# One row buffer in place of two in a fused attention and expert block: the load of the rows, their statistics and four orders in the queues moved

## The chip, the cores and the metric

One core of one Trainium2 chip runs the whole program in one launch. The metric is the device time of an execution in microseconds (us), the median of the runs. The engines are TensorE (PE; PEld is its weight load), VectorE (DVE), ScalarE (ACT), GpSimd (POOL) and SyncE (SP), which here issues all transfers.

## The reference, cut to what matters

```python
x = x + tanh(g_xattn) * attention(layernorm(x), ctx)      # x: 16 batches of 256 rows, 512 wide; 16 heads of 32, causal
x = x + tanh(g_ffn) * experts(layernorm(x))               # softmax router, top 6 of 8 experts, plus a shared one
```

The kernel computes float32 products in three passes over high and low parts, so each operand that TensorE reads is written twice: a high part by ACT and the difference (the low part) by DVE or POOL.

## The kernel before, in words

The program has two halves. The attention half goes through the 16 batches in passes i = -1 to 16; the expert half follows from about 600 us on, and its first steps are woven into passes 14, 15 and 16. The change lies in the attention half.

**A pass.** Each pass has 16 slots s, one per head. Every engine runs the same double loop over passes and slots and does in each slot what its own list says; semaphores tie the engines together. Pass i computes the scores and the softmax of batch i (one head a slot), projects q, k and v for batch n = i + 1, finishes the output projection and the residual of batch o = i - 1, and loads and normalises the rows x of batch ln = i + 2. In order of the slots, as far as they matter here:

- SP: `turn` (L413) issues one transposing transfer of a head's probabilities a slot, two slots late. In slot 0 it stores the finished x1 of batch i - 2 (L424; in pass 16 this is in slot 2), in slot 1 it loads x of batch ln (L438, `X_LOAD`), in slot 2 x of batch o again as the residual (L433, `RES_LOAD`), in slot 9 the context (L445).
- PE: slots 0 and 2 transpose the normalised x of batch n (L780 from `x_in` or `x_odd`), slots 4 to 7 project q, 8 to 11 v, 12 to 15 the output (L790); every fourth slot has the scores of four heads (L896) and the values of four (L916 to L918).
- DVE: in slots 0, 4, 8 and 12 the maxima of four heads (L720), in slot 5 the statistics of x (L622 to L635: `bn_stats`, `bn_aggr` and four small instructions that end in a first guess of 1/std), in slot 6 a low part of q (L740) and the closing of four heads (L673, L674, L678), in slot 10 a rest of v (L728), another closing and the normalising of x (L642), in slot 11 the low part of the transposed values (L660), for which PE's output projection in slot 12 waits.
- ACT: a cast (L592) and two exponentials (L598) a head, and the high parts.
- POOL: a low part of the probabilities a head, one slot late (L488, "split" below), in slot 6 the residual plus bias (L504, two instructions), in slot 7 the eleven small steps that refine 1/std (L81, L83, "Newton steps" below, `NEWTON_SLOT`), in slots 11 and 13 a third part of v (L493).

**Two buffers.** x of even batches goes to `x_odd`, of odd ones to `x_in`. The load of batch ln therefore waits only for the transposes of batch i, which PE did in the pass before. `x_odd` lies in memory that later belongs to the experts; POOL (pass 15, slot 3) and ACT (pass 15, slot 1) wait for two semaphores before they write there for the experts: `scores_done` of batch 14 and `v3_made` of batch 15.

Pass -1 has its own list of slots (`First`): PE transposes batch 0 in slots 5 and 6, DVE has the statistics of batch 1 in slot 8.

Of the kernel before, what the change touches and what calls it, by code (L numbers as in the profile page):

```python
# [15 lines left out]
P = 128  # L16
# [84 lines left out]
class Attended(NamedTuple):  # L101
# [13 lines left out]
    pv_done: object  # L115
    v3_made: object

# [68 lines left out]
def attention(nc, ctx, memory, x, ctx_t, g_xattn, g_ffn, wq_t, wk_t, wv_t, wo_t, bo, x1, x1t, done, ident, gates, tanh_gates):  # L186
# [24 lines left out]
    even = heads_of(0)  # L211
    x_odd = sb("x_odd", [P, T, D])
    sb("experts_space", [P, 2 * JH * C * S - D - T * D])

    def x_of(n):
        return x_in if n.k % 2 else x_odd

    v_rest = [sb("v_rest0", [P, D])]
# [47 lines left out]
    x1_stored, x1t_stored, x1_made, x_hat_made, hat_t_made, scores_done, o_done, v_done = done[:8]  # L266
    q_done, xt_done, c_lo_made, max_made, pv_done, v3_made = done[8:]
    row_chain, guess2_made, pool_chain2 = sem("row_chain"), sem("guess2_made"), sem("pool_chain2")
# [3 lines left out]
    small_loaded = sem("small_loaded")  # L272
    x_loaded, c_loaded, res_loaded = [sem("even_x_loaded"), sem("odd_x_loaded")], sem("c_loaded"), sem("res_loaded")

    ident_made, mask_made, bias_made = sem("ident_made"), sem("mask_made"), sem("bias_made")
    pool_chain, rstd_made = sem("pool_chain"), sem("rstd_made")
    res_made = sem("res_made")
# [51 lines left out]
    X_T_LOADS = (1, 4, 6, 8)  # L329
    X_LOAD, RES_LOAD, C_LOAD, GATE_LOAD, ROWS_LOAD = 1, 2, 9, 12, 13  # L330
    LN_SLOT, NEWTON_SLOT, XN_SLOT = 5, 7, 10
    K_SLOTS, K_EVAC = (0, 1, 2, 3), (2, 4)
# [46 lines left out]
    def phase(i):  # L379

        return i.k - (B - 2)
# [3 lines left out]
    def build(start):  # L385
        def sync(sp):
            sp.dma_start(c_in[:], c_v[0]).then_inc(c_loaded, DMA)
            for n in range(N_RAW):
                src = w_v[RAW_ORDER[n // 2]][:, :, (n % 2) * HD:(n % 2 + 1) * HD]
                sp.dma_start(raw[n], src).then_inc(raw_loaded[n], DMA)  # L390
                if n == 1:
                    sp.dma_start(x_of(At(0, 2, 0))[:], x_v[0]).then_inc(x_loaded[0], DMA)
                    sp.dma_start(gates[:, 0:1], g_xattn.partition_broadcast(P)).then_inc(small_loaded, DMA)
                    sp.dma_start(gates[:, 1:2], g_ffn.partition_broadcast(P)).then_inc(small_loaded, DMA)
                    sp.dma_start(bias[:], bo.partition_broadcast(P)).then_inc(small_loaded, DMA)
# [20 lines left out]
            def run(i):  # L416
                n, o, ln = i + 1, i + -1, i + 2
                k = hat_tile(i + -1)
                for s in range(H):
                    if (bh := lagging(i, s, TURN_LAG)):  # L420
                        turn(head(*bh))
                    if s == (2 if is_end(i) else 0) and has(i, -2):
                        sp.wait_ge(x1_made, (i + -2).times(T, T))
                        sp.dma_start(row(x1_v, i + -2), x_res[:]).then_inc(x1_stored, DMA)  # L424
                    if s == 2 and k is not None and k % T == T - 1:
                        store_hat(k // T)
                    if s in X_T_LOADS and phase(i) == 0:
                        start.sync(sp, phase(i), X_T_LOADS.index(s))
# [7 lines left out]
                    if s == X_LOAD and has(i, 2):  # L436
                        wait(sp, xt_done, ln.times(T, -T))
                        sp.dma_start(x_of(ln)[:], row(x_v, ln)).then_inc(x_loaded[ln.k % 2], DMA)  # L438
                    if s == 3 and phase(i) == 2:
                        start.sync(sp, phase(i), 1)  # L440
# [10 lines left out]
        def gpsimd(pool):  # L451
# [30 lines left out]
            def run(i):  # L482
                n, o, ln = i + 1, i + -1, i + 2
                for s in range(H):
# [16 lines left out]
                    if s == RES_SLOT and has(i, -1):  # L501
                        pool.wait_ge(res_loaded, o.times(DMA, DMA))
                        for t in range(T):
                            pool.tensor_tensor(x_res[:, t, :], x_res[:, t, :], bias[:], ALU.add).then_inc(res_made, 1)  # L504
                    if s == (NEWTON_SLOT if i.k >= 0 else places(i).moments) and has(i, 2):
                        inverse_std(ln)
# [107 lines left out]
        def vector(dve):  # L614
# [3 lines left out]
            def statistics(ln):  # L618

                dve.wait_ge(x_loaded[ln.k % 2], DMA * (ln.k // 2 + 1))  # L620
                for t in range(T):
                    dve.bn_stats(stats[:, t, :], x_of(ln)[:, t, :]).then_inc(norm_chain, 1)  # L622
                dve.wait_ge(norm_chain, ln.times(NORM_STEPS, T))
# [14 lines left out]
            def normalise(ln):  # L638

                dve.wait_ge(rstd_made, ln.times(1, 1))  # L640
                for t in range(T):
                    dve.tensor_scalar(x_of(ln)[:, t, :], x_of(ln)[:, t, :], mv[:, t, 0:1], rstd[:, t:t + 1],  # L642
                                      ALU.subtract, ALU.mult).then_inc(xn_made, 1)
# [129 lines left out]
        def tensor(pe):  # L773
# [40 lines left out]
            def units(i, s):  # L814
                n, o = i + 1, i + -1
                first = isinstance(n.r, int) and n.k == 0
                if has(i, 1):
# [14 lines left out]
                    if s in places(i).x:  # L832
# [4 lines left out]
                        if t == 1:  # L837
                            pe.wait_ge(xt_lo_made, n.times(T, 1))
                        transpose_rows(lambda c: x_of(n)[:, t, c * P:(c + 1) * P], rows_ps).then_inc(xt_done, 1)
                    if s in places(i).q:  # L840
# [101 lines left out]
def experts(nc, ctx, x1, x1t, done, router, w_gate, w_up, w_down, out, ident, tanh_gates):  # L942
# [27 lines left out]
    x1_stored, x1t_stored, x1_made, x_hat_made, hat_t_made, scores_done, o_done, v_done = done[:8]  # L970
    q_done, xt_done, c_lo_made, max_made, pv_done, v3_made = done[8:]

# [398 lines left out]
    def start_gpsimd(pool, phase, s):  # L1371
# [4 lines left out]
        elif (phase, s) == (1, 3):  # L1376
            pool.wait_ge(scores_done, H * (B - 1))
            pool.wait_ge(v3_made, GROUPS * B)
            x_lo_by(pool, 0, B11)
# [18 lines left out]
    def start_scalar(act, phase, s):  # L1398
        if (phase, s) == (1, 1):
            act.wait_ge(scores_done, H * (B - 1))  # L1400
            act.wait_ge(v3_made, GROUPS * B)
            weights_hi(act, 0, (W_A,))
# [477 lines left out]
```

## Time and profile before

| what | value |
|---|---|
| median of 3 runs | 1864.12 us (1862.8 to 1864.49) |
| profiled execution, its own time | 1864.49 us |
| its span, first to last instruction | 1862.7 us |
| busy: PE, PEld, DVE, ACT, POOL | 96%, 80%, 76%, 52%, 50% of the span |
| mean granted TensorE clock | 0.986 of full |

The profile is of one execution. Its span is 1.8 us shorter than the time of the same execution. A busy share is a mean over two halves with different limits, so it is read by stretch.

### The profile page before, as it was taken

Reading aid. Unit: us, or ns where it says so; the run is one execution under the profiler, and the core shown is the slowest. Engines: PE = TensorE matmul, PEld = TensorE weight load, DVE = VectorE, ACT = ScalarE, POOL = GpSimd, SP = SyncE. Lnnn points to the kernel's source line nnn. Section 1 sums busy time; section 2 is a strip of 40 time slices with the busy share of each in tenths; the row PEclk is TensorE's granted clock in tenths of the full one; section 3 lists DMA queues with packets and bytes.
Section 4 is the critical chain, followed back from the end, with each engine's and each line's share of the span. In section 5 each row is a group of like instructions: output and inputs, shape, how many; then the busy total and the mean of one; then the engine's idle time right before and its main releaser. Section 6 shows DMA issues by size and latency. Waiting matters only on the chain.

```text
span 1862.7 us, 33757 instructions
## 1 busy us (share of the span) xinstructions
PE 1788.4 (96%) x11904; PEld 1494.0 (80%) x11904; DVE 1419.7 (76%) x3101; ACT 965.2 (52%) x2260; POOL 925.8 (50%) x1185
## 2 busy tenths in 40 slices
PE   6999999999997999999999999999999999999999
PEld 6878888878885778888778888878888887888887
DVE  5787777777779777777877777787777788777776
ACT  4888888888888433333534243343333444333431
POOL 4776777777678333443533334434343452333330
PEclk9999999999997999999999999999999999999999
DMA  5678887887887412121141221123212113211111
GB/s 157 129 151 166 151 169 160 167 156 144 182 170 145 146 57 80 46 80 46 46 147 46 80 71 54 52 73 113 80 46 80 45 57 106 87 46 57 46 46 46
DMA packets 301000, 182.84 MB, mean 98 GB/s; under 512 B 210080, under 2 KB 265376, under 8 KB 300832
## 3 DMA queue, kind: packets, MB, share of 16 engines
q1 hardware_dynamic: 300832, 180.69, 39.3%
q8 instruction: 95, 1.56, 0.3%
q14 instruction: 73, 0.60, 0.1%
HBM read 111.43 MB, written 18.87 MB: 70 GB/s over the span
## 4 chain that ended last, share of the span: by engine, by line
PE 70%; DVE 11%; POOL 9%; issue 6%; ACT 2%; DMA 1%; SPq 0%; DVEq 0%; POOLq 0%; ACTq 0%
PE gate_up L1293 31%; PE down L1810 18%; PE bank L790 14%; POOL halves L488 3%; DVE ops_lo L1150 2%; DVE acc L1661 2%; PE scores L896 2%; POOL hidden L1509 1%; PE y_values L918 1%; POOL x_res L504 1%; PE rows_t L780 1%; PE y_values L916 1%; DVE xo_lo L1095 1%; PE down L1774 1%; PE down L1789 1%
## 5 line engine op out<-in xcount | busy, mean ns | idle before, releaser
L1293 PE MATMUL gate_up<-xo_hi,ops_hi 128*128 128x512 f32 x1120 | 439.9, 393 | 13.0 <-DVE hidden L1269 4.4
L1293 PE MATMUL gate_up<-xo_lo,ops_hi 128*128 128x512 f32 x1120 | 436.1, 389 | 0.0
L1293 PE MATMUL gate_up<-xo_hi,ops_lo 128*128 128x512 f32 x1120 | 436.0, 389 | 0.0
L488 POOL TENSOR_TENSOR halves<-probs,halves 128x384 f16<-128x384 f32 x244 | 228.8, 952 | 88.9 <-ACT halves L592 88.7
L1661 DVE SCALAR_TENSOR_TENSOR acc<-down,scale,acc 128x512 f32<-128x512 f32 x320 | 238.2, 745 | 34.8 <-PE down L1810 34.3
L1293 PEld LDWEIGHTS gate_up<-xo_hi,ops_hi 128*128 128x128 f32 x1120 | 210.2, 188 | 66.6 <-DVE gated L1269 9.5
L598 ACT ACTIVATE probs<-probs,neg_max 128x128 f32<-128x128 f32 (+1 forms) x512 | 228.9, 449 | 44.4 <-DVE neg_max L720 44.3
L1509 POOL TENSOR_TENSOR hidden<-hidden,gated 128x512 f32<-128x512 f32 x120 | 157.2, 1318 | 190.0 <-DVE hidden L1274 170.5
L1810 PE MATMUL down<-d_hi,h_hi 128*128 128x512 f32 x640 | 249.1, 389 | 0.0
L1810 PE MATMUL down<-d_lo,h_hi 128*128 128x512 f32 x640 | 249.1, 389 | 0.0
L1810 PE MATMUL down<-d_hi,h_lo 128*128 128x512 f32 x640 | 249.0, 389 | 0.0
L1293 PEld LDWEIGHTS gate_up<-xo_lo,ops_hi 128*128 128x128 f32 x1120 | 210.2, 188 | 44.1
L1293 PEld LDWEIGHTS gate_up<-xo_hi,ops_lo 128*128 128x128 f32 x1120 | 210.3, 188 | 42.4
L1544 ACT CAST h_hi<-hidden 128x512 fp32r<-128x512 f32 x160 | 95.3, 621 | 199.1 <-DVE hidden L1646 118.6
L1159 POOL TENSOR_TENSOR w_sums<-u_raw 128x256 f32<-128x256 f32 x40 | 29.5, 737 | 320.1 <-DVE ops_lo L1150 314.0
L1252 ACT COPY first<-gate_up 128x512 f32<-128x512 f32 x80 | 47.0, 587 | 260.9 <-PE gate_up L1293 260.9
L720 DVE CUSTOM_DVE_ANT_0 probs<-scores,mask 128x128 f32<-128x128 f32 (+1 forms) x512 | 147.3, 351 | 29.4 <-PE scores L896 26.1
L1533 ACT ACTIVATE gated<-gated 128x512 f32<-128x512 f32 x120 | 75.8, 632 | 147.9 <-DVE gated L1274 116.2
L1159 POOL TENSOR_TENSOR w_sums<-g_raw 128x256 f32<-128x256 f32 x40 | 36.6, 916 | 224.0 <-DVE ops_lo L1150 223.8
L1650 DVE TENSOR_TENSOR h_lo<-hidden,h_hi 128x512 fp32r<-128x512 f32 x160 | 117.3, 750 | 33.0 <-ACT h_hi L1544 32.8
L1810 PEld LDWEIGHTS down<-d_hi,h_hi 128*128 128x128 f32 x640 | 120.1, 188 | 25.3
L1810 PEld LDWEIGHTS down<-d_hi,h_lo 128*128 128x128 f32 x640 | 120.1, 188 | 25.0
(186 smaller groups left out, 4262.8 us busy)
## 6 DMA issues: line engine op xcount, KB each, us to landing
g_raw<-in_w_gate SPq DMA_DIRECT2D x40, 512.0 KB, 3.5
u_raw<-in_w_up SPq DMA_DIRECT2D x40, 512.0 KB, 3.5
d_raw<-in_w_down SPq DMA_DIRECT2D x40, 512.0 KB, 3.5
c_in<-in_ctx_t SPq DMA_DIRECT2D x16, 512.0 KB, 4.5
x_res<-in_x SPq DMA_DIRECT2D x16, 512.0 KB, 5.6
x_between<-x_res SPq DMA_DIRECT2D x16, 512.0 KB, 3.4
acc<-x_between SPq DMA_DIRECT2D x32, 256.0 KB, 4.4
out<-acc SPq DMA_DIRECT2D x32, 256.0 KB, 3.3
```

The lines of the kernel that those rows point to most:

```text
L488: pool.tensor_tensor(halves[k % HALVES][:, 1, :], probs[k % RING][:], halves[k % HALVES][:, 0, :], ALU.subtract).then_inc(p_lo_made, 1)
L598: ins = act.activation(p, p, ACT.Exp, bias=neg_max[:, s, t:t + 1], scale=-1.0, accum_out=row_sum[:, s, t:t + 1])
L720: ins = dve.tensor_tensor_reduce(probs_of(k, t), scores_of(k, t), mask[:, P * (1 - t):], -SCALE, -NEG, ALU.add, ALU.min, neg_max[:, h, t:t ...
L790: ins = pe.matmul(dst, stationary[a](c), moving[b](c), start=(c == 0 and k == 0), stop=(c == C - 1 and k == len(PASSES) - 1))
L1159: pool.tensor_tensor(w_sums[:, 0], a21, a22, ALU.add).then_inc(w_sum_made, 1)
L1293: ins = pe.matmul(gu_ps[bank][:], ops[x][:, which, a, c, :], xo[y][:, b, c, :], start=(begins and c == 0 and i == 0), stop=(c == CH - 1 an ...
L1509: pool.tensor_tensor(hidden[:, blk, :], hidden[:, blk, :], gated[:, blk, :], ALU.mult).then_inc(gated_made, 1)
L1533: act.activation(gated[:, blk, :], gated[:, blk, :], ACT.Silu).then_inc(silu_made, 1)
L1544: act.copy(h_hi[:, blk, :], hidden[:, blk, :]).then_inc(h_hi_made, 1)
L1650: dve.tensor_tensor(h_lo[:, blk, :], hidden[:, blk, :], h_hi[:, blk, :].bitcast(F32), ALU.subtract).then_inc(h_lo_made, 1)
L1661: dve.scalar_tensor_tensor(out=part, in0=ring("down", m, t)[:], scalar=scale[:, q, t, e:e + 1], in1=part, op0=ALU.mult, op1=ALU.add).then_ ...
L1810: ins = pe.matmul(ring(*use)[:], h[x][:, FC * g + f, t * P:(t + 1) * P], (d_hi, d_lo)[y][m % 2][:, f, :], start=(f == 0 and i == 0), stop= ...
```

## The change

- `x_odd` and its semaphore go; all batches use `x_in`. The memory around it stays where it was.
- SP issues the load of x of batch i + 2 in slot 3 behind the residual's load, where it was in slot 1 ahead of it, and waits before it for the transposes of batch i + 1, PE's slot 2 of the same pass.
- The statistics of x move from slot 5 to slot 7 of DVE. POOL's Newton steps stay in slot 7 (in pass -1 both stay in slot 8).
- In pass 16 the store of x1 of batch 14 moves from slot 2 to slot 0 of SP, that is, between the last two `turn`s.
- ACT and POOL no longer wait themselves for `v3_made` and `scores_done` in pass 15. SP does, in slot 1 after its `turn`, and then raises `early_free`, for which they wait.

```diff
-    x_odd = sb("x_odd", [P, T, D])
-    sb("experts_space", [P, 2 * JH * C * S - D - T * D])
-    def x_of(n):
-        return x_in if n.k % 2 else x_odd
+    sb("experts_space", [P, 2 * JH * C * S - D])
...
-    X_LOAD, RES_LOAD, C_LOAD, GATE_LOAD, ROWS_LOAD = 1, 2, 9, 12, 13
-    LN_SLOT, NEWTON_SLOT, XN_SLOT = 5, 7, 10
+    RES_LOAD, X_LOAD, C_LOAD, GATE_LOAD, ROWS_LOAD = 2, 3, 9, 12, 13
+    LN_SLOT, XN_SLOT = 7, 10
...
-                    if s == (2 if is_end(i) else 0) and has(i, -2):
+                    if s == 0 and has(i, -2):
                         sp.wait_ge(x1_made, (i + -2).times(T, T))
                         sp.dma_start(row(x1_v, i + -2), x_res[:]).then_inc(x1_stored, DMA)
...
+                    if s == 1 and is_last(i):
+                        sp.wait_ge(v3_made, T * B)
+                        sp.wait_ge(scores_done, H * (B - 1))
+                        sp.sem_inc(early_free, 1)
...
                     if s == X_LOAD and has(i, 2):
-                        wait(sp, xt_done, ln.times(T, -T))
-                        sp.dma_start(x_of(ln)[:], row(x_v, ln)).then_inc(x_loaded[ln.k % 2], DMA)
-                    if s == 3 and phase(i) == 2:
+                        sp.wait_ge(xt_done, ln.times(T))
+                        sp.dma_start(x_in[:], row(x_v, ln)).then_inc(x_loaded, DMA)
+                    if s == X_LOAD and phase(i) == 2:
...
-                    if s == (NEWTON_SLOT if i.k >= 0 else places(i).moments) and has(i, 2):
+                    if s == places(i).moments and has(i, 2):
                         inverse_std(ln)
...
-            pool.wait_ge(scores_done, H * (B - 1))
-            pool.wait_ge(v3_made, GROUPS * B)
+            pool.wait_ge(early_free, 1)
             x_lo_by(pool, 0, B11)
...
-            act.wait_ge(scores_done, H * (B - 1))
-            act.wait_ge(v3_made, GROUPS * B)
+            act.wait_ge(early_free, 1)
             weights_hi(act, 0, (W_A,))
```

## Rows read from the trace of the kernel before

**Rows 1.** The page: the chain that ended last, by engine.

```profile
PE 70%; DVE 11%; POOL 9%; issue 6%; ACT 2%; DMA 1%; SPq 0%; DVEq 0%; POOLq 0%; ACTq 0%
```

**Rows 2.** Windows: length, busy PE, PEld, DVE, ACT, POOL, clock, DMA share, GB/s.

```profile
182.97:219.58 36.61, 34.91 (x406) 30.71 (x406) 28.15 (x105) 30.04 (x96) 27.43 (x48) 0.95 0.92 157
219.58:254.73 35.15, 33.47 (x406) 29.66 (x406) 28.19 (x105) 29.96 (x96) 27.43 (x48) 1.00 0.79 148
```

**Rows 3.** Waits in 0 to 640 us: total, times, longest.

```profile
PE bank L790 <- DVE t_lo L660: 21.8, 15, 1.7
...
POOL x_res L504 <- DMA x_res<-in_x: 4.5, 2, 4.0
```

**Rows 4.** Timeline of pass 3, DVE: start, duration, what, [idle before <- releaser].

```profile
152.87 0.17 DVE L629 TENSOR_SCALAR var_eps<-mv 128x2 f32<-128x2 f32 x1
...
153.35 0.68 DVE L740 TENSOR_TENSOR q_lo<-bank,q_hi 128x512 fp32r<-128x512 f32 x1
...
154.74 1.06 DVE L678 TENSOR_TENSOR y<-y_sum,row_inv 128x256 f32<-128x256 f32 x1
156.21 0.29 DVE L720 CUSTOM_DVE_ANT_0 probs<-scores,mask 128x128 f32<-128x128 f32 x1 [0.41 <-PE scores L896]
...
162.54 0.91 DVE L678 TENSOR_TENSOR y<-y_sum,row_inv 128x256 f32<-128x256 f32 x1
163.38 2.19 DVE L642 TENSOR_SCALAR x_in<-x_in,mv,rstd 128x512 f32<-128x512 f32 x2
165.49 0.68 DVE L660 TENSOR_TENSOR t_lo<-rows_t,t_hi 128x512 fp32r<-128x512 f32 x1
```

**Rows 5.** The same pass on ACT.

```profile
156.89 0.41 ACT L598 ACTIVATE probs<-probs,neg_max 128x128 f32<-128x128 f32 x1 [0.36 <-DVE neg_max L720]
...
160.53 0.58 ACT L556 CAST v_parts<-bank 128x512 bf16<-128x512 f32 x1 [0.59 <-PE bank L790]
```

**Rows 6.** The same pass on POOL.

```profile
156.91 0.92 POOL L488 TENSOR_TENSOR halves<-probs,halves 128x384 f16<-128x384 f32 x1
157.79 0.20 POOL L83 TENSOR_TENSOR newton<-rstd 128x2 f32<-128x2 f32 x1
...
161.37 3.92 POOL L488 TENSOR_TENSOR halves<-probs,halves 128x384 f16<-128x384 f32 x4
```

**Rows 7.** PE's output projection in pass 3.

```profile
166.22 0.50 PE L790 MATMUL bank<-w_hi,t_hi 128*128 128x512 f32 x1 [1.66 <-DVE t_lo L660]
```

**Rows 8.** Pass 14, which has no statistics, on DVE.

```profile
547.48 1.52 DVE L678 TENSOR_TENSOR y<-y_sum,row_inv 128x256 f32<-128x256 f32 x1
```

**Rows 9.** Pass 2, whose slot 8 is late, on ACT and DVE.

```profile
123.56 0.40 ACT L598 ACTIVATE probs<-probs,neg_max 128x128 f32<-128x128 f32 x1 [1.96 <-DVE neg_max L720]
...
126.22 0.57 ACT L556 CAST v_parts<-bank 128x512 bf16<-128x512 f32 x1
...
129.31 1.59 DVE L642 TENSOR_SCALAR x_odd<-x_odd,mv,rstd 128x512 f32<-128x512 f32 x2
```

**Rows 10.** The tile `x_in`: durations in ns, min/median/max, first and last start.

```profile
L642 DVE TENSOR_SCALAR x_in<-x_in,mv,rstd x16: 535/1132/1352, 37.2 to 523.0; 128x512 f32<-128x512 f32 x16
...
DMA to landing us min/median/max: 4.3/5.0/8.7
```

**Rows 11.** SP's `turn` in slot 3 of pass 3.

```profile
147.28 1.21 SPq L413 DMA_TRANSPOSE turned<-halves  x1
```

**Rows 12.** Pass 15 on ACT, SP and PE.

```profile
570.65 0.60 ACT L1140 CAST ops_hi<-g_raw 128x512 fp32r<-128x512 f32 x1
...
573.96 1.56 SPq L413 DMA_TRANSPOSE turned<-halves  x1
...
582.27 1.12 PE L780 MATMUL rows_t<-ident,y 128*128 128x128 f32 x4 [2.46 <-DVE y L678]
...
589.43 0.80 PE L790 MATMUL bank<-w_hi,t_hi 128*128 128x512 f32 x1 [1.06 <-DVE t_lo L660]
```

**Rows 13.** PE's wait for the last transposed head, in pass 16.

```profile
606.50 0.20 PE L916 MATMUL y_values<-v_parts,turned 128*128 128x64 bf16 x1 [2.43 <-DMA turned<-halves]
```

More of the change, by code:

```diff
@@ L115 @@
     pv_done: object
-    v3_made: object
+    early_free: object
 class Slots(NamedTuple):
@@ L266, in attention @@
     x1_stored, x1t_stored, x1_made, x_hat_made, hat_t_made, scores_done, o_done, v_done = done[:8]
-    q_done, xt_done, c_lo_made, max_made, pv_done, v3_made = done[8:]
+    q_done, xt_done, c_lo_made, max_made, pv_done, early_free = done[8:]
     row_chain, guess2_made, pool_chain2 = sem("row_chain"), sem("guess2_made"), sem("pool_chain2")
@@ L272, in attention @@
     small_loaded = sem("small_loaded")
-    x_loaded, c_loaded, res_loaded = [sem("even_x_loaded"), sem("odd_x_loaded")], sem("c_loaded"), sem("res_loaded")
+    x_loaded, c_loaded, res_loaded = sem("x_loaded"), sem("c_loaded"), sem("res_loaded")
     ident_made, mask_made, bias_made = sem("ident_made"), sem("mask_made"), sem("bias_made")
-    pool_chain, rstd_made = sem("pool_chain"), sem("rstd_made")
+    pool_chain, rstd_made, v3_made = sem("pool_chain"), sem("rstd_made"), sem("v3_made")
     res_made = sem("res_made")
@@ L391, in sync @@
                 if n == 1:
-                    sp.dma_start(x_of(At(0, 2, 0))[:], x_v[0]).then_inc(x_loaded[0], DMA)
+                    sp.dma_start(x_in[:], x_v[0]).then_inc(x_loaded, DMA)
                     sp.dma_start(gates[:, 0:1], g_xattn.partition_broadcast(P)).then_inc(small_loaded, DMA)
@@ L618, in statistics @@
             def statistics(ln):
-                dve.wait_ge(x_loaded[ln.k % 2], DMA * (ln.k // 2 + 1))
+                dve.wait_ge(x_loaded, ln.times(DMA, DMA))
                 for t in range(T):
-                    dve.bn_stats(stats[:, t, :], x_of(ln)[:, t, :]).then_inc(norm_chain, 1)
+                    dve.bn_stats(stats[:, t, :], x_in[:, t, :]).then_inc(norm_chain, 1)
                 dve.wait_ge(norm_chain, ln.times(NORM_STEPS, T))
@@ L641, in normalise @@
                 for t in range(T):
-                    dve.tensor_scalar(x_of(ln)[:, t, :], x_of(ln)[:, t, :], mv[:, t, 0:1], rstd[:, t:t + 1],
+                    dve.tensor_scalar(x_in[:, t, :], x_in[:, t, :], mv[:, t, 0:1], rstd[:, t:t + 1],
                                       ALU.subtract, ALU.mult).then_inc(xn_made, 1)
@@ L838, in units @@
                             pe.wait_ge(xt_lo_made, n.times(T, 1))
-                        transpose_rows(lambda c: x_of(n)[:, t, c * P:(c + 1) * P], rows_ps).then_inc(xt_done, 1)
+                        transpose_rows(lambda c: x_in[:, t, c * P:(c + 1) * P], rows_ps).then_inc(xt_done, 1)
                     if s in places(i).q:
@@ L970, in experts @@
     x1_stored, x1t_stored, x1_made, x_hat_made, hat_t_made, scores_done, o_done, v_done = done[:8]
-    q_done, xt_done, c_lo_made, max_made, pv_done, v3_made = done[8:]
+    q_done, xt_done, c_lo_made, max_made, pv_done, early_free = done[8:]
     x_t = sb("x_t", [P, GROUPS, C, BLK])
```

## The prediction

> **What bounds the kernel now.** I read the page first: PE is busy 96% of the span, and most of the chain that ended last is PE's work, with DVE and POOL behind it [rows 1]. Such a chain says that PE is the bound with short waits in between, so the waits come next: in the attention half PE's one wait that comes back pass after pass is that of the output projection for the low part of the transposed values, 15 times up to 1.7 us [rows 3, 7]. The windows say what the rest of a pass is: about 35 us long and PE busy nearly throughout; in 5 of the 12 passes 2 to 13 the clock is 0.95 and the pass 1.5 us longer [rows 2]. In those five the clock falls to 1.2 GHz right behind that wait and comes back. So this change is priced by one question: when does DVE write that low part (L660), measured against PE?
>
> I then follow pass 3 back from it. L660 stands behind the normalising, 163.38 to 165.57; that behind a closing at 162.54; that behind ACT's high part of v at 160.53, for which ACT waited 0.59 us for PE [rows 4, 5]. ACT's exponential of slot 8 at 156.89 waited for DVE's maxima, which began at 156.21, 0.68 earlier, and these waited 0.41 for PE's scores [rows 4, 5]. Between slots 7 and 8 DVE thus has 0.41 us of air, and ACT 0.59 us behind it. In slot 5, where the statistics stand now, DVE's next work is a low part whose source ACT had finished 0.5 us before it began: air for a quarter of the 2.2 us.
>
> **The steady passes, step by step.** The statistics leave slot 5 and the low part of q begins 0.5 us earlier. That brings nothing, because the closing behind it ends in the multiplication L678, which is held by POOL's residual additions: in pass 14, with no statistics at all, it begins 0.46 us earlier in its pass and takes 1.52 us where pass 3 has 1.06 [rows 4, 8]: the end is the same. So in pass 3 it still ends at 155.80, and the statistics follow from 155.72 (neighbours overlap by 0.08).
>
> Their small instruction L629 comes 1.73 us after the start of the statistics, at 157.45. POOL is then in a split, 156.91 to 157.83 [rows 6]. DVE instructions of this kind are held until POOL's ends, as the second of pass 3's normalisings shows: 2.19 us for two that take 0.535 each at best [rows 4, 10]. So L629 ends at about 157.85, and the maxima begin 0.31 later as now from its end (153.04) to the next work (153.35) [rows 4]: 158.16 for 156.21, 1.95 us late. If POOL did not hold it, 1.7.
>
> ACT's exponential begins at 158.84. From there to the high part of v ACT needs 2.66 us if it waits for nothing, which pass 2 shows, where slot 8 was late already (123.56 to 126.22) [rows 9]. That gives 161.50 for 160.53: 0.97 late, the air taken off. The closing's multiplication, 2.01 behind it, is ready at 163.50 for 162.54. POOL's Newton steps begin when the guess is there, 158.35 for 157.79, and their four splits begin 3.58 later, at 161.93 for 161.37 [rows 6]. Splits and DVE's instructions now take turns: the multiplication gets in when the second split ends (163.73) and ends at 164.0; the third split ends at 164.8; the first normalising ends at 165.07; the fourth split, ready at 164.86, goes next and ends at 165.85; the second normalising ends at 166.13. L660 follows, and PE begins at 166.79 for 166.22: 0.57 us a pass. Only part of the 0.97 comes through, since DVE loses less to POOL than now. The bounds: 0.97 if it loses as much; and if the second normalising gets in ahead of the fourth split, as in pass 2 (1.59 us for both) [rows 9], L660 is at 165.4 and the pass gains 0.1. I take 0.57, as the fourth split is ready 0.2 us before the first normalising ends.
>
> The Trainium skill (SBUF — State Buffer, Who interferes with whom) has the rule behind this: VectorE and GpSimd share a port pair that is held for a whole instruction, and whichever issues first gets it. By it the fourth split goes first here too, but two instructions of VectorE back to back could keep the pair, and the sum would then lose its 6.3 us below.
>
> Passes with this shape are 1, 3 to 9 and 11 to 13: 11 x 0.57 = 6.3 us. Pass 2 is partly there already: 0.3. Pass 10 is late now from a wait of POOL for the residual's load, which the new order issues earlier [rows 3]; I count it as no change. Pass 0 has no output projection: 0.3, between 0 and 0.57. In pass -1 SP's new wait ends with PE's slot 6, ahead of DVE's slot 8; nothing. Sum 6.9; bounds -1.3 and 12.
>
> **The load.** It is issued behind SP's `turn` of slot 3, which ends at 148.5 in pass 3 [rows 11]; the transposes it waits for are over by then in every pass from 0 on (PE's slot 2). With 5.0 us to landing, at most 8.7 [rows 10], it is there at 153.5, and the statistics want it at 155.72: hidden under 2.2 us. The queue behind it, `turn`s of slots 4 and later, gains 0.7 us in slots 2 and 3 and loses it after; heads 0 to 3 are wanted in slot 9.
>
> **Pass 15.** ACT casts its first expert weights at 570.65. `early_free` comes after SP's `turn` in slot 1, issued from 573.96 to 575.52 [rows 12], because that `turn` waits for POOL's and DVE's splits and stands behind the store of x1. ACT stands still for 4.9 us. Behind it are its casts and exponentials of all later slots, and for them DVE's splits, SP's `turn`s and PE's transposes wait. ACT had hardly any air up to slot 11: PE's output projection at 589.43 waited for L660 and thus for ACT. I take 4.3 us; the bounds are 2.6, what I get by way of DVE's split of slot 6 to PE's transposes at 582.27, which waited for DVE already [rows 12], and 4.9. POOL's slot 3 is later than 575.5 and waits for nothing.
>
> **Pass 16.** The store of x1 now stands between the last two `turn`s: 0.6 us of issue and 512 KB ahead of the last head's transfer, for which PE already waits 2.43 us [rows 13]. All of it shows: 1.0 us, between 0.6 and 2.
>
> **The clock.** PE's wait grows from 1.7 to 2.3 us, and in pass 15 there is more idle time; I expect one more fall, 1.5 us, between none and eight (12 us, every pass).
>
> Sum: 6.9 + 4.3 + 1.0 + 1.5 = 13.7. Against the profiled execution's own 1864.49 (0.4 above the median, which I leave in) that is 1878.
>
> **Rivals.**
> - *Both costs as above*: 1878, with its own range 1873 to 1884. Chance 0.60.
> - *The full 0.97 comes through and the clock falls in half of the other passes or more*: 11 x 0.97 = 10.7 + 0.6 + 5.3, and 4 to 8 falls: 1887 to 1893. For it: the wait comes near what pass 15 has, where the clock is low; against: passes with 1.7 us escape 7 times of 12. 0.12.
> - *The load lands late* in the eight passes where DMA is busiest (share 0.92 at most) [rows 2]: a us each, 1886. The Trainium skill (DMA: Bandwidth & Descriptors, Rules for kernel authors) says to issue early and wait late, which the change does the other way; the rows above leave it 2.2 us of cover. 0.05.
> - *Only the end costs*: the second normalising slips in ahead of the fourth split, each pass gains 0.1: 1864.5 - 1.1 + 5.3 = 1869. 0.10.
> - *Nothing shows*: that, and ACT's stall is caught up before 589: 1864.5 - 1.1 + 1.0, 1864. 0.06.
> - *Faster*: both normalisings find POOL waiting for ACT's casts. Decided by whether the third split ends before the first normalising is ready (163.9; I have 164.8). They would take 1.1 instead of 2.19 us: 12 x 1.1 = 13.2 gained, 5.3 lost: 1857. 0.07.
>
> **How the numbers follow.** No change can be told from one below 0.2% (3.7 us). Slower: 0.60 + 0.12 + 0.05 + 0.10 = 0.87; same 0.06; faster 0.07. The range from 1867 to 1889 leaves out the last two cases and the upper half of the second.
>
> **What would show it.** In pass 3's counterpart: DVE's maxima of slot 8 follow the statistics with no wait, 1.9 us later in the pass; ACT waits some 2 us before the exponential of slot 8; PE's wait for L660 is 2.2 to 2.3 us; passes 35.2 us long, or 36.7 with a fall. In pass 15 ACT's first expert cast has 4.9 us of idle time before it. In pass 16 PE's wait for the last head is 3 us or more. I am wrong if PE's wait stays 1.7 us, or if the time lies in the first passes or in the expert half.

## The result and the profile after

| kernel | median | runs | ratio to before, 95% interval |
|---|---|---|---|
| before | 1862.8 us | 1858.96 to 1864.49, 5 runs | |
| after | 1873.6 us | 1871.63 to 1873.64, 5 runs | 1.0056 [1.0042, 1.0072] |

The change makes the kernel slower by 0.56%, 10.4 us by the ratio (the two medians are 10.8 apart). The prediction had 1878 in a range from 1867 to 1889. The profiled execution of after has a span of 1869.7 us, that of before 1862.7. These two are only 7.0 us apart: the profiled execution of after took 1871.45 us, less than any of its five in the table, that of before 1864.49, the most of its five, so what is read from the two traces adds up to less than the medians.

The page of after, the chain that ended last, by engine, as in [rows 1]:

```profile
PE 69%; DVE 15%; issue 6%; ACT 4%; POOL 3%; DMA 2%; SPq 1%; DVEq 0%; POOLq 0%; ACTq 0%
```

Windows of passes 4 and 5 of after, columns as in [rows 2]:

```profile
182.93:218.65 35.72, 33.71 (x406) 29.52 (x405) 28.09 (x105) 29.89 (x96) 27.48 (x47) 1.00 0.85 158
218.65:254.40 35.75, 33.78 (x406) 29.57 (x405) 28.68 (x105) 29.74 (x96) 27.41 (x48) 1.00 0.82 155
```

Waits of after from 0 to 640 us, as in [rows 3]:

```profile
PE bank L789 <- DVE t_lo L659: 16.7, 15, 1.3
...
PE bank L789 <- DVE q_lo L739: 10.9, 13, 1.6
```

Two things are to be seen. Each pass is 0.6 us longer than its counterpart (35.75 for 35.15), yet pass 4 is 0.9 us shorter than before, since its clock doesn't fall; none of the passes 1 to 13 has a fall now, and five had one before. And the wait for the low part of the transposed values has shrunk to 1.2 us, while a new one has come, for the low part of q. The waits together grew by 0.3 us a pass; the other 0.3 shows as busy time of PE (33.78 for 33.47 us, the same 406 products), and no run says why.

Pass 3 of after, timeline of DVE, the counterpart of [rows 4]:

```profile
153.57 1.51 DVE L677 TENSOR_TENSOR y<-y_sum,row_inv 128x256 f32<-128x256 f32 x1
155.00 1.27 DVE L621 BATCH_NORM_STATS2 stats<-x_in 128x6 f32<-128x512 f32 x2
...
156.73 0.41 DVE L628 TENSOR_SCALAR var_eps<-mv 128x2 f32<-128x2 f32 x1
...
157.57 0.29 DVE L719 CUSTOM_DVE_ANT_0 probs<-scores,mask 128x128 f32<-128x128 f32 x1
...
159.80 0.69 DVE L739 TENSOR_TENSOR q_lo<-bank,q_hi 128x512 fp32r<-128x512 f32 x1
...
162.90 0.43 DVE L677 TENSOR_TENSOR y<-y_sum,row_inv 128x256 f32<-128x256 f32 x1
163.24 2.22 DVE L641 TENSOR_SCALAR x_in<-x_in,mv,rstd 128x512 f32<-128x512 f32 x2
165.38 0.68 DVE L659 TENSOR_TENSOR t_lo<-rows_t,t_hi 128x512 fp32r<-128x512 f32 x1
```

The same pass on ACT, POOL and PE, as in [rows 5 to 7]:

```profile
158.25 0.40 ACT L597 ACTIVATE probs<-probs,neg_max 128x128 f32<-128x128 f32 x1 [2.43 <-DVE neg_max L719]
...
160.91 0.56 ACT L555 CAST v_parts<-bank 128x512 bf16<-128x512 f32 x1
...
157.62 0.20 POOL L83 TENSOR_TENSOR newton<-rstd 128x2 f32<-128x2 f32 x1 [0.51 <-DVE rstd L634]
...
161.22 2.88 POOL L487 TENSOR_TENSOR halves<-probs,halves 128x384 f16<-128x384 f32 x3
164.26 0.92 POOL L487 TENSOR_TENSOR halves<-probs,halves 128x384 f16<-128x384 f32 x1 [0.16 <-ACT halves L591]
...
160.54 0.50 PE L789 MATMUL bank<-w_hi,c_hi 128*128 128x512 f32 x1 [0.75 <-DVE q_lo L739]
...
166.12 0.50 PE L789 MATMUL bank<-w_hi,t_hi 128*128 128x512 f32 x1 [1.23 <-DVE t_lo L659]
```

Pass 3 of after began 0.72 us earlier (maxima of slot 4 at 147.59 for 148.31), so 0.72 is added to compare. The maxima of slot 8 are then 2.08 us late, the exponential 2.08, the high part of v 1.10, PE's output projection 0.62.

The end of the attention half, passes 15 and 16 of after, on ACT, SP and PE, as in [rows 12, 13]:

```profile
574.26 0.62 ACT L1139 CAST ops_hi<-g_raw 128x512 fp32r<-128x512 f32 x1 [4.88 <-SPq L425]
...
571.92 0.57 SPq L419 DMA_DIRECT2D x_between<-x_res  x1
572.60 3.00 SPq L408 DMA_TRANSPOSE turned<-halves  x2
...
605.69 0.57 SPq L419 DMA_DIRECT2D x_between<-x_res  x1
606.37 1.56 SPq L408 DMA_TRANSPOSE turned<-halves  x1
...
583.33 0.47 PE L779 MATMUL rows_t<-ident,y 128*128 128x128 f32 x1 [4.43 <-DVE y L677]
...
592.91 0.79 PE L789 MATMUL bank<-w_hi,t_hi 128*128 128x512 f32 x1 [1.31 <-DVE t_lo L659]
...
612.05 0.20 PE L915 MATMUL y_values<-v_parts,turned 128*128 128x64 bf16 x1 [4.38 <-DMA turned<-halves]
...
621.93 0.47 PE L1292 MATMUL gate_up<-xo_hi,ops_hi 128*128 128x512 f32 x1 [1.16 <-DVE xo_lo L1094]
```

To read the end apart from the passes, both kernels are measured from the same instruction, the first maxima of slot 4 of pass 14. In after:

```profile
540.31 0.29 DVE L719 CUSTOM_DVE_ANT_0 probs<-scores,mask 128x128 f32<-128x128 f32 x1 [1.18 <-PE scores L895]
```

In before, with the first product of the expert half on PE:

```profile
541.51 0.29 DVE L720 CUSTOM_DVE_ANT_0 probs<-scores,mask 128x128 f32<-128x128 f32 x1 [1.18 <-PE scores L896]
...
615.03 0.47 PE L1293 MATMUL gate_up<-xo_hi,ops_hi 128*128 128x512 f32 x1 [1.42 <-DVE xo_lo L1095]
```

After reaches pass 14 sooner than before, by 1.2 us. From there the output projection of pass 15 comes 52.6 us on for 47.9, the first product of the experts 81.6 for 73.5, the end of the span 1329.4 for 1321.2. So in this pair of traces all of the loss lies from pass 14 on: 8.2 us, of which the earlier start of pass 14 gives 1.2 back. The experiments show how much of that is the change, and why the longer passes don't show.

### The profile page after: what moved, and what is told of

Its sections match the earlier page's. It is cut to its first block, busy times and chain, and to the rows that moved or that the text cites. A ratio compares the mean times of both kernels' runs of the same rounds, so it can differ in the third digit from the quotient of the medians.

```text
span 1869.7 us, 33758 instructions
## 1 busy us (share of the span) xinstructions
PE 1785.5 (95%) x11904; PEld 1488.6 (80%) x11904; DVE 1420.5 (76%) x3101; ACT 963.3 (52%) x2260; POOL 926.1 (50%) x1185
## 4 chain that ended last, share of the span: by engine, by line
PE 69%; DVE 15%; issue 6%; ACT 4%; POOL 3%; DMA 2%; SPq 1%; DVEq 0%; POOLq 0%; ACTq 0%
PE gate_up L1292 32%; PE down L1807 19%; PE bank L789 13%; DVE ops_lo L1149 2%; DVE acc L1658 2%; ACT probs L597 2%; POOL hidden L1506 1%; PE scores L895 1%; DVE y L677 1%; DVE x_in L641 1%; PE y_values L917 1%; DVE stats L621 1%; PE rows_t L779 1%; PE y_values L915 1%; DVE y_sum L673 1%
## 5 line engine op out<-in xcount | busy, mean ns | idle before, releaser
L1807 PEld LDWEIGHTS down<-d_lo,h_hi 128*128 128x128 f32 x640 | 120.1, 188 | 25.1
```

The lines of the kernel that those rows point to most:

```text
L1807: ins = pe.matmul(ring(*use)[:], h[x][:, FC * g + f, t * P:(t + 1) * P], (d_hi, d_lo)[y][m % 2][:, f, :], start=(f == 0 and i == 0), stop= ...
```

## The experiments

All times are medians, each kernel run beside the kernel before on the same chip. "To the end" is the stretch of the profiled execution from the maxima of slot 4 of pass 14 to the end of the span.

| run | what it is | ratio, 95% interval | to the end |
|---|---|---|---|
| e1_end_only | before, both end edits | 1.0040 [1.0027, 1.0053] | 1330.2 |
| e2_stats_only | before, statistics in slot 7 | 1.0005 [0.9997, 1.0014] | 1322.7 |
| e3_after_direct_wait | after without `early_free` | 1.0023 [1.0014, 1.0032] | 1324.1 |
| e4_before_normalise_11 | before, normalising in slot 11 | 0.9915 [0.9901, 0.9928] | 1323.6 |
| e5_after_store_late | after, store of x1 in slot 2 | 1.0041 [1.0029, 1.0053] | 1328.5 |
| e6_load_order | before, load of x moved alone | 1.0123 [1.0108, 1.0137] | 1322.5 |
| e7_single_wait_longer | before, more DVE work in slot 10 | 1.0014 [1.0002, 1.0026] | 1321.9 |
| e8_after_no_end_normalise_11 | after, no end edits, normalising in 11 | 0.9978 [0.9970, 0.9987] | 1323.5 |
| e9_after_no_end | after, no end edits | 1.0019 [1.0010, 1.0028] | 1322.6 |
| e10_split_wait | before, more DVE work in slot 8 | 0.9997 [0.9988, 1.0006] | 1323.1 |
| e11_before_normalise_12 | before, normalising in slot 12 | 0.9917 [0.9904, 0.9931] | 1323.1 |
| e12_one_buffer_8_12 | one buffer, slots 8 and 12 | 0.9940 [0.9928, 0.9952] | 1326.8 |

### The end against the passes

`e1_end_only` and `e2_stats_only` put one part each into the kernel before. First e1, whose two edits are shown one below the other (ACT and POOL wait for `early_free`, as in after), then e2:

```diff
+                    if s == 1 and is_last(i):
+                        sp.wait_ge(v3_made, T * B)
+                        sp.wait_ge(scores_done, H * (B - 1))
+                        sp.sem_inc(early_free, 1)
...
-                    if s == (2 if is_end(i) else 0) and has(i, -2):
+                    if s == 0 and has(i, -2):
```
```diff
-    LN_SLOT, NEWTON_SLOT, XN_SLOT = 5, 7, 10
+    LN_SLOT, NEWTON_SLOT, XN_SLOT = 7, 7, 10
```

> The kernel before (two buffers, load and statistics where they were) with the two edits at the end of the attention half alone: SP raises early_free in slot 1 of pass 15, and the store of x1 in pass 16 stands between the last two turns. My theory now, from the profile after: these two carry all of the loss, because ACT stands still for 4.9 us before its first expert cast and PE waits 2 us longer for the last head. It expects 7 to 8.5 us over before, the first maxima of pass 14 where they are in the kernel before. Rival A, that the steady passes carry it (my forecast put 6.9 us there), expects 4 to 5.5 us over before. Rival B, that the end only costs in company of the later passes, expects under 2.

> The kernel before with one number changed: the statistics of x in slot 7 of DVE in place of slot 5; two buffers and the early load stay. Theory: this alone makes the steady pass of the kernel after, 35.2 us without and 35.8 us with the second layernorm's work (34.7 and 35.2 before), since L660 is 0.6 us later; PE's one wait of 1.7 us becomes two, 0.75 and 1.2 us, and the clock stops falling, which gives 5 x 1.5 us back. So the time is within 2 us of before, and the first maxima of pass 14 come at 540 to 542 us. Rival A, the clock falls are chance and come back: 6 to 8 us over before. Rival B, the later load and not the statistics makes the pass longer: pass length as before, 34.7 us, and the time within 1 us.

Measured: 1871.69 and 1864.76 us. The end edits alone are 7.5 us, with the same stall of ACT (4.87 us for 4.88) and the same wait of PE for the last head (4.30 for 4.38) as in after. The statistics alone are within 0.2% of before. But their passes show the price in full, 35.25 and 35.72 us, and PE's two waits:

```profile
PE bank L790 <- DVE t_lo L660: 16.3, 15, 1.2
...
PE bank L790 <- DVE q_lo L740: 9.8, 13, 0.9
```

Thirteen passes at 0.6 are paid back by the clock, which falls in none of the passes 1 to 13. This is not the luck of one trace: over all runs the mean granted clock is 0.991 in the 11 of e2 and 0.986 in the 21 of before beside it. The difference is 0.0046 of the span, 8.6 us of full clock, and five falls of 3.4 us at half speed are 8.5.

### Which end edit

`e3_after_direct_wait` takes `early_free` out of after (the edit of ACT is shown, POOL has the same), `e5_after_store_late` puts the store back:

```diff
-            act.wait_ge(early_free, 1)
+            act.wait_ge(scores_done, H * (B - 1))
+            act.wait_ge(v3_made, GROUPS * B)
```
```diff
-                    if s == 0 and has(i, -2):
+                    if s == (2 if is_end(i) else 0) and has(i, -2):
```

> The kernel after, with ACT and POOL waiting themselves for scores_done and v3_made in pass 15, and no early_free. Theory: ACT's 4.9 us of standing still go, PE's output projection of pass 15 comes 4.7 us earlier against pass 14, and the kernel gains 4.5 to 5.5 us on after. Rival A, PE's low clock in pass 15 and DVE's backlog make that up: a gain of 1 to 3 us. Rival B, the stall was on no path: no gain.

> The kernel after, with the store of x1 in pass 16 back in slot 2, behind the last head's transfer; early_free stays. Theory: the store's issue and bytes ahead of the last transfer cost what PE's wait for the last head grew by, 4.38 for 2.43 us in the kernel after (the first run of the end edits alone had 4.30). So that wait goes back to 2.4 to 2.8, and the time falls by 2 us against the kernel after, to about 1.0045 of before; the stall of 4.9 us before ACT's first expert cast stays. Rival: the wait for the last head grew because the whole chain of pass 15 to 16 is late and the transfers collide with others: then it stays above 4 us and the time stays at 1.0056 of before, within 0.1%.

Measured: 1868.19 and 1872.24 us. Without `early_free` ACT goes straight on (no idle time stands in its row) and the wait for the last head stays; with the late store it is the other way round. ACT and PE of `e3_after_direct_wait`:

```profile
571.73 0.60 ACT L1136 CAST ops_hi<-g_raw 128x512 fp32r<-128x512 f32 x1
...
609.41 0.24 PE L912 MATMUL y_values<-v_parts,turned 128*128 128x64 bf16 x1 [4.27 <-DMA turned<-halves]
```

The same of `e5_after_store_late`:

```profile
576.88 0.62 ACT L1139 CAST ops_hi<-g_raw 128x512 fp32r<-128x512 f32 x1 [4.88 <-SPq L425]
...
612.96 0.20 PE L915 MATMUL y_values<-v_parts,turned 128*128 128x64 bf16 x1 [2.67 <-DMA turned<-halves]
```

The two costs are apart: the early store makes the last wait (4.3 to 4.4 us with it in e1, e3 and after, 2.4 to 2.7 without it in before, e5 and e9), whatever came before it. With `e9_after_no_end`, where both are undone, four corners are measured:

> The kernel after with both edits at the end undone: ACT and POOL wait themselves for what early_free stood for, and in pass 16 the store of x1 is in slot 2. What is left is the steady part: one buffer, the load in slot 3 behind the transposes, the statistics in slot 7. Theory: the end edits alone gave 1.0040 and the statistics in slot 7 alone 1.0005, the kernel after 1.0056; what remains for the load in slot 3 is 0.0011, 2 us, which is pass 6, where x lands late. So 1865 to 1867, ratio 1.0005 to 1.0015, passes of 35.25 and 35.75 us and no or one fall of the clock in passes 1 to 14. Rival: the steady part costs what the prediction had, 8 us with the clock: 1872.

It came out at 1866.24 us, within the theory's times, its ratio just above them. To the end it is 1322.6 with neither, 1324.1 with the early store, 1328.5 with `early_free`, 1329.4 with both: about 1.2 us for the store and 5.6 for `early_free`. By the ratios the store is 0.7 to 2.8 us and `early_free` 4.1 to 6.1, and the steady part of the change, which alone is left here, costs 3.5 us (1.9 to 5.2).

### The load alone

```diff
-    X_LOAD, RES_LOAD, C_LOAD, GATE_LOAD, ROWS_LOAD = 1, 2, 9, 12, 13
+    X_LOAD, RES_LOAD, C_LOAD, GATE_LOAD, ROWS_LOAD = 3, 2, 9, 12, 13
...
-                        wait(sp, xt_done, ln.times(T, -T))
+                        wait(sp, xt_done, ln.times(T))
```

> The kernel before with two buffers, statistics in slot 5; only the load of x moves, to slot 3 behind the residual's load and behind the transposes of slot 2. Theory: the residual's load gains what x's load loses, the statistics in slot 5 begin 4 us after the load's issue and would now wait for it: landing 5 to 6 us after 148.5 in pass 3 is 153.5 to 154.5, while the statistics begin at about 151. So here the order alone does cost: DVE waits 2 to 3 us in slot 5 in every pass, of which PE has 0 to 2 us, 1865 to 1885. That gives the price of a load that lands late, which in the kernel after the statistics in slot 7 avoid in all passes but 6. Rival: DVE has air in slots 5 and 6 and the time stays within 0.1% of before.

Measured: 1887.58 us, just above the theory's bound. Pass 3 on SP, DVE and PE:

```profile
152.15 0.57 SPq L438 DMA_DIRECT2D x_in<-in_x  x1
...
157.09 1.29 DVE L622 BATCH_NORM_STATS2 stats<-x_in 128x6 f32<-128x512 f32 x2 [2.66 <-DMA x_in<-in_x]
...
158.83 1.15 DVE L629 TENSOR_SCALAR var_eps<-mv 128x2 f32<-128x2 f32 x1
...
161.70 0.50 PE L790 MATMUL bank<-w_hi,c_hi 128*128 128x512 f32 x1 [2.49 <-DVE q_lo L740]
```

DVE waits 2.66 us for x, a small instruction behind it takes 1.15 for 0.17 us, and PE waits 2.49 us for the low part of q. Passes 3 to 13 are 37.0 to 38.1 us, and the clock falls in 12 of the passes 1 to 13. The statistics in slot 7 are thus no extra cost but what makes the late load bearable: without them the steady part of the change would cost 23 us.

### Is the clock set by the length of the wait?

Two kernels give DVE more work in the kernel before, e7 ahead of the normalising, e10 behind the maxima of slot 8:

```diff
+                    if s == places(i).normal and has(i, 0) and has(i, 2):
+                        dve.bn_stats(unused[:], x_of(ln)[:, 0, :])
```
```diff
+                    if s == 8 and has(i, 0) and has(i, 2):
+                        for t in range(T):
+                            dve.bn_stats(unused[:, t, :], x_of(ln)[:, t, :])
```

> The kernel before with one more bn_stats of half of x, into a tile that nothing reads, ahead of the normalising in slot 10 (passes 0 to 14 that normalise). The output stays the reference's. PE's wait for the low part of the transposed values grows by 0.7 us, from 1.7 to 2.3 or 2.4, as one wait. In the kernel after the idle time is the same in sum but lies in two waits of 0.75 and 1.2 us, and the clock falls in none of passes 1 to 14. Theory: the single wait is what lets the clock fall in 5 passes of before; a longer single wait then falls in as many passes or more (5 to 12), and the time is 14 x 0.65 = 9 us plus 0 to 10 us: 1873 to 1883. Rival: whether the clock falls does not hang on the length of this wait: no more than 5 falls, and 1868 to 1873.

> The kernel before with more work and nothing else: two bn_stats of x into a tile that nothing reads, 1.2 us of DVE ahead of the low part of q in slot 8, in passes 0 to 13. The output stays the reference's. DVE has 1.43 us of idle time behind that low part and the next one, before the rest of v. Theory: PE must wait 0.5 to 0.7 us for the bank of v's second half, what comes behind it on DVE is where it was, and PE's later wait for the low part of the transposed values shrinks by the same: two waits of 0.6 and 1.1 us in place of one of 1.66, passes as long as before (34.65 and 35.15), and the clock then falls in none or one of passes 1 to 14, where before has 4 to 6 falls of 1.5 us: 1856 to 1859, faster for more work. Rival: the clock does not hang on how the waits are cut, and falls 4 to 6 times as before: 1862 to 1866. Second rival: the idle time is not there, and each pass grows by 0.3 or more: 1868 or more.

Measured: 1866.58 and 1862.43 us. Both theories missed (1873 to 1883 and 1856 to 1859), because neither kernel did to PE's wait what it was made for, so neither settles the question by itself. In e7 the extra instruction was nearly free. DVE in its pass 3:

```profile
161.61 0.93 DVE L679 TENSOR_TENSOR y<-y_sum,row_inv 128x256 f32<-128x256 f32 x1
162.46 0.68 DVE L768 BATCH_NORM_STATS2 unused<-x_in 128x6 f32<-128x512 f32 x1
163.06 1.59 DVE L643 TENSOR_SCALAR x_in<-x_in,mv,rstd 128x512 f32<-128x512 f32 x2
164.58 0.68 DVE L661 TENSOR_TENSOR t_lo<-rows_t,t_hi 128x512 fp32r<-128x512 f32 x1
```

The two normalisings take 1.59 for 2.19 us [rows 4]: what DVE had lost to POOL's splits was filled with work, and the low part comes as early as before. PE's wait stays 1.68 in pass 3 and about 1.7 in most others; only in passes 8 and 9 was it longer, 2.48 in both, and the clock fell in the second alone. That is good evidence for the step of the prediction by which lateness ahead of the normalising is partly swallowed, since the splits set its end. In e10 the wait was cut in passes 3 (0.61 and 0.74 us) and 4 (0.20 and 0.88), with no fall there; in the eleven others one wait of about 1.5 us stayed, and the clock fell in four of them. The second rival of e10, that there is no idle time to use, is out: 1.2 us more of work a pass cost nothing.

What bears on it most is all traces together. For passes 1 to 13 of the 14 kernels, the longest wait of PE in the pass, and whether the clock falls in it:

| longest wait of PE in the pass | passes | with a fall |
|---|---|---|
| up to 1.3 us | 114 | 0 |
| 1.3 to 2.0 us | 51 | 17 |
| over 2.0 us | 17 | 15 |

So up to 1.3 us the clock never fell here, and above 2.0 nearly always. Between them the length doesn't decide: in before, the five passes with a fall had waits of 1.63 to 1.71 us, seven without one 1.65 to 1.70. What decides among those is open.

### A better place for the normalising

The first edit is of the kernel before (e4; in e11 the last number is 12), the second of after with both end edits undone (e8; in e12 the numbers are 8 and 12):

```diff
-    LN_SLOT, NEWTON_SLOT, XN_SLOT = 5, 7, 10
+    LN_SLOT, NEWTON_SLOT, XN_SLOT = 5, 7, 11
```
```diff
-    LN_SLOT, XN_SLOT = 7, 10
+    LN_SLOT, XN_SLOT = 7, 11
```

> The kernel before with the normalising of x in slot 11 of DVE, behind the low part L660, in place of slot 10, ahead of it. A measure of what PE's steady wait for L660 is worth. Theory: L660 begins 2.1 us earlier, PE's wait of 1.7 us falls below 0.3 us in passes 1 to 13 and with it the five falls of the clock: 13 x 1.5 + 5 x 1.5, 22 to 28 us under before. Rival A, the maxima of slot 12 are then late and PE waits for ACT elsewhere: 5 to 12 us under before. Rival B, the clock falls stay although the wait is gone: 17 to 20 us.

> One buffer, load in slot 3, statistics in slot 7 as in the kernel after; the two edits at the end undone (ACT and POOL wait themselves, the store of x1 in slot 2), and the normalising in slot 11 of DVE behind the low part of the transposed values, which in the kernel before alone gave 0.9915. Theory: the statistics in slot 7 then cost what they did to the high part of v and q_lo: PE's wait for the second bank of v (0.75) stays and the rest is gone, so some 0.2 to 0.5 us a pass over the run with the normalising moved in the kernel before: 1850 to 1855, ratio 0.993 to 0.995. Rival: with the normalising away DVE's queue has air that takes the statistics in: 1847 to 1849, the same as there.

> The kernel before with the normalising of x in slot 12 of DVE, behind the maxima and the rest of v of that slot; in slot 11, between the low part of the transposed values and the maxima, it gave 0.9915 and left PE short waits of 0.2 to 0.7 us for the rest of v in seven passes. Theory: these go, the maxima of slot 12 are 1.6 us earlier, and it gains 1 to 4 us more: 1844 to 1847. Rival: the output's residual and the closing behind it are late then, and it gives that back: 1848 to 1852.

> One buffer and the load in slot 3 as in the kernel after, both edits at the end undone, and two other slots: the statistics (and with them POOL's Newton steps) in slot 8 of DVE, behind the low parts of q and of the transposed values, where DVE stood idle for 1.43 us before the rest of v; the normalising in slot 12 behind the rest of v. With two buffers, statistics in slot 5 and the normalising in slot 12 the ratio was 0.9917; with one buffer, statistics in slot 7 and the normalising in slot 11 it was 0.9978. Theory: it was the place of the statistics, ahead of the maxima of slot 8, that cost the latter kernel its gain (PE's wait of 0.75 us for the low part of q, and the exponential of slot 8 late), and not the single buffer: maxima of slot 8 and that low part are on time again, 1.4 of the 2.2 us lie in idle time, the rest of v is up to 0.8 us late and PE waits 0 to 0.5 us for it: 1848 to 1855, ratio 0.992 to 0.9955. Rival: the Newton steps, later by 2 us, push POOL's four splits behind them, and with them the transfers of the heads, and PE waits for these: 1858 or more.

Measured: 1847.69, 1860.18, 1846.99 and 1852.14 us. e4 met none of its forecasts: it gained 16 us where 22 to 28 were expected, since PE keeps short waits in other passes (up to 0.7 us, and pass 10 is 35.2 us long). e8 missed both of its own by 5 us and more. With the low part of the transposed values ahead of the normalising, PE doesn't wait for it. Pass 3 of e4 on DVE, then its window:

```profile
161.28 0.69 DVE L660 TENSOR_TENSOR t_lo<-rows_t,t_hi 128x512 fp32r<-128x512 f32 x1
161.88 1.60 DVE L642 TENSOR_SCALAR x_in<-x_in,mv,rstd 128x512 f32<-128x512 f32 x2
```
```profile
146.10:179.30 33.20, 33.20 (x402) 29.25 (x402) 28.66 (x105) 28.94 (x94) 25.49 (x40) 1.00 0.89 158
```

PE is busy 33.20 of 33.20 us, and the clock falls in no pass from 1 to 13. Slot 12 (e11) is no better than slot 11: the gain of 1 to 4 us more did not come. In e8, the statistics in slot 7 hold the passes at 35.0 us, some 1 us a pass over e4 where 0.2 to 0.5 was expected. PE's waits there:

```profile
PE bank L786 <- DVE q_lo L736: 10.9, 13, 1.8
...
PE bank L786 <- DVE v_rest L724: 5.1, 13, 0.7
```

In e12 they stand in slot 8, in DVE's idle time. DVE in pass 3:

```profile
161.10 0.69 DVE L736 TENSOR_TENSOR q_lo<-bank,q_hi 128x512 fp32r<-128x512 f32 x1
161.70 1.28 DVE L618 BATCH_NORM_STATS2 stats<-x_in 128x6 f32<-128x512 f32 x2
```

From pass 1 to pass 14 (slot 4 to slot 4) e12 takes 443.1 us, e4 and e11 442.6. So the single buffer with its late load costs nothing in the passes once the statistics stand there; it was their place (e12 moves the normalising to slot 12 too, which between e4 and e11 made no difference). What e12 loses is 5.5 us in pass 0 (37.3 for 31.7) and 3 to 4 from pass 14 on, 2.2 of them in pass 14 itself, which no run explains. In pass 0 POOL waits for the first guess and its work for the context queues behind; PE waits 4.74 for 2.35 us. POOL and PE of e12:

```profile
57.47 0.19 POOL L83 TENSOR_TENSOR newton<-rstd 128x2 f32<-128x2 f32 x1 [3.47 <-DVE rstd L631]
...
70.56 0.58 PE L786 MATMUL bank<-c_hi,w_hi 128*128 128x256 f32 x1 [4.74 <-POOL c_lo L476]
```

Something like the rival of e12 thus holds for that pass alone, by way of the context's low part and not of the heads' transfers. The best kernels are e11 and e4, 16 us faster than before; the best with one buffer is e12, 11 us faster.

## Why the prediction was right, and where it was off

The direction and the range held. The likeliest case, both costs together, is what came, 4.4 us less than forecast. Of these, 1.7 us lie in the base: the sum began at 1864.49, and the median of before is 1862.8. The rest is two errors of opposite sign, a steady part too dear (8.4 us for 3.5 in e9) and an end too cheap (5.3 for 7.5 in e1). That the total came so near is partly luck.

**The steady passes: right.** The prediction's times of pass 3 are 158.16 for the maxima, 158.84 for the exponential, 161.50 for the high part of v, 158.35 for the Newton steps, 161.93 for the splits, 166.13 for the end of the normalising, 166.79 for PE. Measured, with the 0.72 us added: 158.29, 158.97, 161.63, 158.34, 161.94, 166.18, 166.84. That the multiplication would end at 164.0 is met too (162.90 + 0.43 + 0.72 = 164.05). The turn-taking with POOL, chosen at 0.57 between -0.1 and 0.97, gave 0.62; pass 3 is 35.27 for 34.66 us and pass 5 35.75 for 35.15, 0.6 longer. The statistics' small instruction was held by POOL as foreseen (0.41 for 0.17 us). By the rule of the Trainium skill (SBUF — State Buffer, Who interferes with whom) whichever of the two engines issues first goes first; here the trace agrees, and the row of the normalisings, 2.22 us for two that take 0.535 each at best, is its price.

**A wait that was overlooked.** The low part of q in slot 8 stands behind the late maxima, and PE waits 0.75 us for it. The prediction followed only the way to the output projection. It changed no total, since the low part of the transposed values still sets when the output projection begins, but it cut one wait of PE in two. So the sign "PE's wait for L660 is 2.2 to 2.3 us" failed: it is 1.23. The other signs in pass 3 and at the end came.

**The clock: wrong in sign.** The step that failed is "PE's wait grows from 1.7 to 2.3 us ... I expect one more fall, 1.5 us". The idle time did grow, by 0.3 us, but as 0.75 and 1.23 us, and neither is long enough to go with a fall. Five falls went, 7.5 us of gain where 1.5 of loss stood. That is the main part of what took the steady part from 8.4 us to the 3.5 of e9, and to the 0.9 of e2. It would take it further: 13 x 0.6 us, 0.9 for pass 6 (below) and five falls back make 1.2, under the 1.9 to 5.2 of e9, and what is missing there stays open. The count of escapes in the prediction, 7 of 12, takes in pass 2, whose wait was 1.31 us and not 1.7; with waits of 1.6 us or more it is 6 of 11 in those passes. The start of the profiled after is also 1.5 us shorter, one more fall that before has at 24.6 us. Seven of the 14 traces have that fall, with the edits at the start and without, so it is not put down to the change.

**The load: nearly hidden.** The rival of a late load had 8 passes at a us each. One came: in pass 6 x landed late.

```profile
262.91 1.29 DVE L621 BATCH_NORM_STATS2 stats<-x_in 128x6 f32<-128x512 f32 x2 [1.02 <-DMA x_in<-in_x]
```

There the load was issued late, at 256.58, 2.2 us behind the maxima of slot 4 where pass 3 has 0.7, and took 6.3 us to land (the median of the tile is now 6.0 us, 5.0 in [rows 10]). In pass 3 the landing took 4.9 us as forecast, and the cover was 1.7 us and not 2.2 only because the `turn` ahead of the load took longer (2.02 us for the 1.21 of [rows 11]): load issued at 148.33, landed at 153.3, wanted at 155.00. The profiled after got off lightly: in the traces of e3, e5 and e9 DVE waits 2.3 to 2.5 us for x in pass 6, and in e3 PE then waits 2.03 us and the clock falls. e6 shows what the rule in the Trainium skill (DMA: Bandwidth & Descriptors, Rules for kernel authors), to issue early and wait late, is worth where the cover is gone: 23 us.

**Pass 15: right, slightly small.** ACT's stall was given as 4.9 us and is 4.88. Of it 4.7 came through to the output projection, for 4.3.

**Pass 16: the store undersized in the trace.** PE's wait grew by 1.95 us, from 2.43 to 4.38, at the upper bound, not by 1.0; e5 gives 1.7 of it back. In the time it is 0.7 to 2.8 us.

**What the sum at the end lacked.** Between the last head and the first product of the experts after loses 1.5 us more, which the prediction put at nothing. The clock is low for longer behind ACT's stall, and falls once more behind the wait for the last head. Windows of after, then of before:

```profile
568.00:598.70 30.70, 16.99 (x206) 14.10 (x207) 21.89 (x71) 25.34 (x79) 23.74 (x20) 0.50 0.68 130
...
612.40:615.80 3.40, 3.40 (x11) 2.67 (x9) 2.92 (x5) 0.58 (x1) 1.62 (x3) 0.51 0.89 308
```
```profile
571.00:594.60 23.60, 14.24 (x176) 11.82 (x173) 21.77 (x67) 23.17 (x73) 22.32 (x20) 0.50 0.76 147
```

In the second window PE is busy throughout at 1.2 GHz, so by estimate it costs half of its 3.4 us, 1.7. This fall is not the change's: of the ten traces of kernels without the end edits or with only the early store, all but e7 and e12 have one such fall of 3.4 us there too, and e12 a longer one; the profiled before happens to have none. With it goes that before's 1321.2 us to the end are 1.4 less than e9's 1322.6. The first window is the change's: 27 to 31 us in the three kernels with `early_free`, some 24 in all others. PE is idle for 13.7 of its 30.7 us, and it ends 5.8 us behind the output projection, where before's ends 5.3 behind; so nearly all of what it costs lies inside the 4.7. So the trace pair has 4.7 + 1.95 + 1.5 = 8.2 us, of which the change has 6.8 (after's 1329.4 against e9's 1322.6), and by e1's ratio 7.5 (5.0 to 9.9), for 5.3 in the prediction.

## What to carry to other kernels

Count a new wait on a queue's engine by what stands behind the waiters: two waits gathered on SP cost 4 to 6 us because SP's program order put them behind a transfer, though what was waited for was there already (in e3 ACT waits for it directly and doesn't stop). Work moved on a busy engine should go where the engine stands idle, not merely where its result is wanted, and the work that another engine waits for should go ahead of work that nobody wants yet: swapping two neighbours on DVE gained 16 us, more than the whole change cost. And where TensorE's clock comes near falling, look not only at the sum of its idle time but at the length of each piece.

## What the runs showed of the hardware

- TensorE's granted clock went with the length of single waits: no fall to 1.2 GHz in 114 passes whose longest wait was up to 1.3 us, a fall in 17 of 51 between 1.3 and 2.0, in 15 of 17 above. A fall costs 1.5 us a pass (36.61 for 35.15). With some 1.9 us of idle time, mostly in two pieces, none of the 26 passes of after and e2 lost it, and of the 39 of e3, e5 and e9 only the one whose wait was 2.03; with 1.7 in one piece 5 of before's 13 did. That the pieces are the cause, and not something that goes with them, no single edit here has shown.
- `bn_stats` with one operand from memory is not held by POOL: 668 to 695 ns in all 32 of after, next to `tensor_scalar` on the same tile with 535 to 1353. The Trainium skill (SBUF — State Buffer, Who interferes with whom) says that a VectorE instruction with at most one such input, outside the two-port modes, doesn't contend; the traces agree. In the shadow of POOL's splits one more of them a pass was nearly free (e7: ratio 1.0014).
- Small instructions aren't safe from POOL: a `tensor_scalar` of 128x2 elements took 1.15 us for 0.17 in e6, beside POOL's residual additions, and ended at 159.98, 0.03 us behind the second of them.
